# One GpSimd power over eight columns for two normalisations, in an attention and feed-forward kernel

## What is computed

```
def _layernorm(x, axis=-1, eps=1e-05):
    m = jnp.mean(x, axis=axis, keepdims=True)
    v = jnp.var(x, axis=axis, keepdims=True)
    return (x - m) / jnp.sqrt(v + eps)
...
q = (x @ Wq.T + bq).reshape(B, S, H, Dh)
v = (x @ Wv.T + bv).reshape(B, S, H, Dh)
...
scores = jnp.einsum('bhsd,bhtd->bhst', q, q) / jnp.sqrt(jnp.float32(E))
same = (b_hs[:, :, :, None] == b_hs[:, :, None, :]).astype(scores.dtype)
coeff = NB - 2 + same
attn = jax.nn.softmax(scores * coeff, axis=-1)
out = jnp.einsum('bhst,bhtd->bhsd', attn, v)
...
x = x + _layernorm(_L0_attn_ref(_layernorm(x, axis=-1), ...), axis=-1)
x = x + _layernorm(_L0_ffn_ref(_layernorm(x, axis=-1), ...), axis=-1)
```

## Time and profile before

| | us |
|---|---|
| median of 3 runs | 1428.81 |
| lowest and highest | 1426.63, 1431.72 |
| the profiled execution | 1425.1 |
| its span, first to last instruction | 1423.3 |
| GpSimd busy | 1257.9 (88%) |
| TensorE busy | 1236.9 (87%) |
| VectorE busy | 1236.4 (87%) |
| ScalarE busy | 1068.1 (75%) |

### The profile page before, as it was taken

One profiled execution on the slowest core, in us unless ns is written; L12 is line 12 of the kernel. 1 busy time (PEld: TensorE's weight loads), 2 busy tenths in 40 slices (PEclk: granted clock), 3 DMA queues, 4 the chain that ended last, 5 costly groups with the idle time before them and its releaser, 6 DMA issues. The chain is left out here.

```text
span 1423.3 us, 19971 instructions
## 1 busy us (share of the span) xinstructions
PE 1236.9 (87%) x5423; PEld 520.1 (37%) x5520; DVE 1236.4 (87%) x4005; ACT 1068.1 (75%) x1461; POOL 1257.9 (88%) x305
## 2 busy tenths in 40 slices
PE   2666799999989999898989999898999989898896
PEld 1111234334343434334343433434343433433343
DVE  3978999999999999999899999999999999999420
ACT  2244787878787887978788787878788797878741
POOL 2689999999999999999999999999999999999810
PEclk9877999999999999999999999999999999999999
DMA  3454345443543555354544544444454545443100
GB/s 99 135 172 127 109 121 152 114 133 113 144 116 115 136 128 137 94 148 117 140 104 128 146 116 135 111 144 117 113 141 116 142 100 142 117 129 92 47 8 8
DMA packets 89377, 167.47 MB, mean 118 GB/s; under 512 B 18096, under 2 KB 54192, under 8 KB 89264
## 3 DMA queue, kind: packets, MB, share of 16 engines
q1 hardware_dynamic: 89264, 166.19, 43.0%
HBM read 150.66 MB, written 15.47 MB: 117 GB/s over the span
## 5 line engine op out<-in xcount | busy, mean ns | idle before, releaser
L901 POOL TENSOR_TENSOR logits<-max_row,logits 128x4096 f32<-128x4096 f32 x128 | 1140.0, 8916 | 47.1 <-DMA max_row<-max_scratch 24.4
L730 DVE CUSTOM_DVE_ANT_0 logits<-s_bank,coeff 128x512 f32<-128x512 f32 x1024 | 692.3, 676 | 0.0
L940 ACT ACTIVATE logits<-logits 128x1024 f32<-128x1024 f32 x512 | 506.2, 1048 | 50.6 <-POOL logits L901 49.2
L695 DVE TENSOR_SCALAR coeff<-brow,bcol 128x516 bf16<-128x516 bf16 x1024 | 480.6, 469 | 54.5 <-PE s_bank L511 26.9
L511 PE MATMUL s_bank<-mov_stack,stat_stack 128*128 128x512 bf16 x927 | 328.4, 395 | 71.3 <-DVE rowmax L730 59.5
L531 PE MATMUL aux_bank<-logits,v_pad 128*32 128x512 f32 x2048 | 252.9, 613 | 31.5 <-ACT logits L940 17.0
L636 PE MATMUL f_bank<-hid_a,h_sb 128*128 128x512 f32 x512 | 248.9, 593 | 1.1 <-DVE hid_a L819 0.8
L511 PEld LDWEIGHTS s_bank<-mov_stack,stat_stack 128*128 128x128 bf16 x1024 | 97.9, 98 | 414.2 <-DVE rowmax L730 215.5
L646 PE MATMUL f_bank<-hid_b,h_sb 128*128 128x512 f32 x512 | 243.5, 593 | 5.0 <-ACT hid_b L1039 3.6
L960 ACT COPY oT<-aux_bank 128x512 f32<-128x512 f32 x64 | 37.5, 586 | 154.7 <-PE aux_bank L531 148.5
L646 PEld LDWEIGHTS f_bank<-hid_b,h_sb 128*128 128x128 f32 x512 | 95.9, 190 | 84.9 <-issue 73.0
(11 more groups left out here) (96 smaller groups left out, 961.3 us busy)
## 6 DMA issues: line engine op xcount, KB each, us to landing
max_row<-max_scratch SPq DMA_DIRECT2D x128, 512.0 KB, 4.1
brow<-bucket_scratch SPq DMA_DIRECT2D x64, 522.0 KB
mov_stack<-q_scratch SPq DMA_DIRECT2D x192, 96.0 KB
stat_stack<-q_scratch SPq DMA_DIRECT2D x192, 96.0 KB
max_scratch<-rowmax_T SPq DMA_DIRECT2D x512, 1.0 KB
q_scratch<-q_parts SPq DMA_DIRECT2D x16, 384.0 KB, 6.5
x_in<-in_x SPq DMA_DIRECT2D x16, 256.0 KB, 4.4
q_scratch<-q_parts SPq DMA_DIRECT2D x16, 256.0 KB, 7.2
```

Of the source, the lines that this page charges most:

```text
L695: nc.vector.tensor_scalar(coeff[:, k % 3, :].rearrange("p (r n) -> p r n", r=ROW_RUNS), brow[:, h // 4 % 2, h % 4, :, 0:RUN], bcol[:, b % ...
L730: nc.vector.tensor_tensor_reduce(out=logits[:, ring(b, k), :], in0=tile_bank(k)[:], in1=coeff[:, k % 3, 0:SEQ], scale=float(E) ** -0.5, sc ...
L901: nc.gpsimd.tensor_tensor(tiles, max_row[:, m % 2].unsqueeze(2).broadcast_to([P, GROUP, ST, SEQ]), tiles, ALU.subtract).then_inc(below_max ...
L940: nc.scalar.activation(logits[:, first:first + 2, :], logits[:, first:first + 2, :], ACT.Exp, scale=-1.0).then_inc(probs_done, 1)
```

## The change

GpSimd no longer takes the power for x at slot 48 and the one for the end at slot 52. It takes one at slot 52, over a tile of 8 columns, of which 0 to 3 are x's and 4 to 7 the end's; the product with the negated means is one over 8 columns too. Where an iteration only prepares or only finishes, the slice has 4 columns. GpSimd waits for both variances ahead of it. ScalarE's x normalise moves from slot 49 to slot 52, behind the exponential of that slot. One count of a semaphore, `xe_bias_done`, stands for both products.

```diff
-X_RSTD_SLOT = 48
-X_NORM_SLOT = 49
+X_RSTD_SLOT = 52
+X_NORM_SLOT = 52
...
-END_RSTD_SLOT = 52
...
-        minus_half = sb("minus_half", [P, ST])
+        minus_half = sb("minus_half", [P, 2 * ST])
...
-        x_var = sb("x_var", [P, ST])
-        x_rstd = sb("x_rstd", [P, ST])
-        x_shift = sb("x_shift", [P, ST])
-        x_bias = sb("x_bias", [P, ST])
+        xe_var = sb("xe_var", [P, 2 * ST])
+        xe_rstd = sb("xe_rstd", [P, 2 * ST])
+        xe_shift = sb("xe_shift", [P, 2 * ST])
+        xe_bias = sb("xe_bias", [P, 2 * ST])
...
-            def rstd(var, shift, out_, bias, prepared, done, bias_done, n):
-
-                pool.wait_ge(prepared, n)
-                nc.gpsimd.tensor_tensor(out_[:], var[:], minus_half[:], ALU.pow).then_inc(done, 1)
+            def rstd(var, shift, out_, bias, done, bias_done, n, part):
+
+                nc.gpsimd.tensor_tensor(out_[:, part], var[:, part], minus_half[:, part], ALU.pow).then_inc(done, 1)
                 pool.wait_ge(done, n)
-                nc.gpsimd.tensor_tensor(bias[:], shift[:], out_[:], ALU.mult).then_inc(bias_done, 1)
+                nc.gpsimd.tensor_tensor(bias[:, part], shift[:, part], out_[:, part], ALU.mult).then_inc(bias_done, 1)
...
-                    if query and k == X_RSTD_SLOT:
-                        rstd(x_var, x_shift, x_rstd, x_bias, x_var_done, x_rstd_done, x_bias_done, p + 2)
-                    if finish and k == END_RSTD_SLOT:
-                        rstd(end_var, end_shift, end_rstd, end_bias, end_var_done, end_rstd_done, end_bias_done, g + 1)
+                    if (query or finish) and k == X_RSTD_SLOT:
+                        if query:
+                            pool.wait_ge(x_var_done, p + 2)
+                        if finish:
+                            pool.wait_ge(end_var_done, g + 1)
+                        part = slice(0 if query else ST, 2 * ST if finish else ST)
+                        rstd(xe_var, xe_shift, xe_rstd, xe_bias, xe_rstd_done, xe_bias_done, i + 3, part)
...
                 if k == X_NORM_SLOT:
-                    act.wait_ge(x_bias_done, p + 1)
-                    normalise(x_in, x_in, x_rstd, x_bias, xn_done)
+                    act.wait_ge(xe_bias_done, p + 1)
+                    normalise(x_in, x_in, xe_rstd, xe_bias, xn_done)
...
                 if slot == END_NORM_SLOT + TILES:
-                    act.wait_ge(end_bias_done, f + 1)
-                    normalise(ffn, ffn, end_rstd, end_bias, end_normed_done)
+                    act.wait_ge(xe_bias_done, f + 5)
+                    normalise(ffn, ffn, xe_rstd[:, ST:2 * ST], xe_bias[:, ST:2 * ST], end_normed_done)
```

More of the change, by code:

```diff
@@ L222, in sandwich_kernel @@
         end_mv = sb("end_mv", [P, ST, 2])
[L223 to L226, removed]
         ynT = sb("ynT", [P, SEQ])
@@ L245, in sandwich_kernel @@
         x_var_done = sem("x_var_done")
-        x_rstd_done = sem("x_rstd_done")
-        x_bias_done = sem("x_bias_done")
+        xe_rstd_done = sem("xe_rstd_done")
+        xe_bias_done = sem("xe_bias_done")
         xn_done = sem("xn_done")
@@ L291, in sandwich_kernel @@
         end_var_done = sem("end_var_done")
-        end_rstd_done = sem("end_rstd_done")
-        end_bias_done = sem("end_bias_done")
         end_normed_done = sem("end_normed_done")
@@ L917, in iteration @@
                         nc.gpsimd.tensor_tensor(ffn[:], ffn[:], y1[:, g % 2], ALU.add).then_inc(y2_done, 1)
-                    if query and k == X_RSTD_SLOT:
-                        rstd(x_var, x_shift, x_rstd, x_bias, x_var_done, x_rstd_done, x_bias_done, p + 2)
-                    if finish and k == END_RSTD_SLOT:
-                        rstd(end_var, end_shift, end_rstd, end_bias, end_var_done, end_rstd_done, end_bias_done, g + 1)
+                    if (query or finish) and k == X_RSTD_SLOT:
[5 more added lines that the diff above has]
+                        rstd(xe_var, xe_shift, xe_rstd, xe_bias, xe_rstd_done, xe_bias_done, i + 3, part)
                     if feed and k == ATT_RSTD_SLOT:
-                        rstd(att_var, att_shift, att_rstd, att_bias, att_var_done, att_rstd_done, att_bias_done, 2 * f + 1)
+                        pool.wait_ge(att_var_done, 2 * f + 1)
+                        rstd(att_var, att_shift, att_rstd, att_bias, att_rstd_done, att_bias_done, 2 * f + 1, slice(0, ST))
                     if feed and k == Y1_RSTD_SLOT:
-                        rstd(att_var, att_shift, att_rstd, att_bias, att_var_done, att_rstd_done, att_bias_done, 2 * f + 2)
+                        pool.wait_ge(att_var_done, 2 * f + 2)
+                        rstd(att_var, att_shift, att_rstd, att_bias, att_rstd_done, att_bias_done, 2 * f + 2, slice(0, ST))
             stages(pool, iteration)
@@ L945, in prepare @@
                 act.wait_ge(ready, n)
-                nc.scalar.activation(var[:], mv[:, :, 1], ACT.Identity, bias=eps[:])
-                nc.scalar.activation(shift[:], mv[:, :, 0], ACT.Identity, scale=-1.0).then_inc(done, 1)
+                nc.scalar.activation(var, mv[:, :, 1], ACT.Identity, bias=eps[:])
+                nc.scalar.activation(shift, mv[:, :, 0], ACT.Identity, scale=-1.0).then_inc(done, 1)
             def normalise(dst, src, rstd, bias, done):
@@ L963, in query_step @@
                 if k == X_PREPARE_SLOT:
-                    prepare(x_mv, x_var, x_shift, x_mv_done, x_var_done, p + 1)
+                    prepare(x_mv, xe_var[:, 0:ST], xe_shift[:, 0:ST], x_mv_done, x_var_done, p + 1)
                 if k == X_NORM_SLOT:
-                    act.wait_ge(x_bias_done, p + 1)
-                    normalise(x_in, x_in, x_rstd, x_bias, xn_done)
+                    act.wait_ge(xe_bias_done, p + 1)
+                    normalise(x_in, x_in, xe_rstd, xe_bias, xn_done)
                 if k == XNT_COPY_SLOT:
@@ L1009, in ffn_step @@
                 if slot == ATT_PREPARE_SLOT:
-                    prepare(att_mv, att_var, att_shift, att_mv_done, att_var_done, 2 * f + 1)
+                    prepare(att_mv, att_var[:], att_shift[:], att_mv_done, att_var_done, 2 * f + 1)
                 if slot == Y1_PREPARE_SLOT:
-                    prepare(att_mv, att_var, att_shift, att_mv_done, att_var_done, 2 * f + 2)
+                    prepare(att_mv, att_var[:], att_shift[:], att_mv_done, att_var_done, 2 * f + 2)
                 if slot == END_PREPARE_SLOT + TILES:
-                    prepare(end_mv, end_var, end_shift, end_mv_done, end_var_done, f + 1)
+                    prepare(end_mv, xe_var[:, ST:2 * ST], xe_shift[:, ST:2 * ST], end_mv_done, end_var_done, f + 1)
                 if slot == ATT_NORM_SLOT:
```

## The result

The changed kernel took 1441.86 us (median of 6 runs, 1440.03 to 1442.41) against 1429.24 before: ratio 1.0094, 95% interval 1.0077 to 1.0111 (the two medians alone give 1.0088). Its profiled execution took 1440.82 us, where the one before took 1425.1. It is slower by 0.9%, where 1.1% was forecast.

A forecast was written before the change was run, and what follows sets the result against it. The prediction took ScalarE, VectorE and DMA, not GpSimd, as the path ahead of the maxima wait. 12 x 1.18 + 0.9 = 15.1 us on 1428.8 gave 1443.9 us, own range 1438 to 1449, wider range 1434 to 1449.

The forecast's parts named there:

- What bounds the kernel: Between about 745 and 771 us the path is ScalarE, VectorE, DMA; GpSimd runs beside it with room.
- Part 1: GpSimd, slots 48 and 52: merged power takes 1.8 us, relieving 5 to 15 us over the run, worth nothing in time.
- Part 2: GpSimd at slot 52 waits for both variances: no wait, 0.8 us to spare.
- Part 3: ScalarE's x normalise, slot 49 to 52: of 1.54 us, 0.36 absorbed before xnT, 1.18 passed on in each of 12 iterations.
- The idle at line 767: VectorE's wait for qT (old line 774) grows from 0.66 to 1.84 us, 12 times; under 1.5 means wrong.
- Part 4: The rest: iteration 1 is 0.9 us late; GpSimd's final addition, iteration 0 and iterations 14 on add nothing.
- The sum: Whole run: 12 x 1.18 + 0.9 = 15.1 us slower, giving 1443.9 us, slower by 1.1%.
- A: GpSimd is the bound, so its saving comes out: 5 to 15 us faster, 1414 to 1424; chance 0.06.
- B: VectorE's late start is absorbed by stalls after 771: 0 to 4 us, 1425 to 1433; chance 0.11.
- C: The lateness is partly absorbed, half of it: 1434 to 1438 us; chance 0.08.
- D: Late transposes of x leave 0.36 unrecovered, scores' lateness adds: 20 us, 1449; within the forecast's 0.75 as its upper end.

The follow-up runs named there:

- relief alone: Kernel before without the end's power and product on GpSimd in iterations 2 to 13, x normalise still at slot 49; 1429.07 us, ratio 0.9999.
- the two powers: Changed kernel with the merged power taken twice, the first into a tile nobody reads; 1444.13 us, ratio 1.0109 to the kernel before.
- the move alone: Kernel before with only ScalarE's x normalise moved from slot 49 to 52, GpSimd keeping its two powers; 1440.28 us, ratio 1.0088.

## Why the prediction was right

- **What bounds the kernel.** Right: GpSimd has the highest busy share and isn't the bound at this place. The run with relief alone shows it from below, the two powers from above. "At this place" matters: behind the maxima wait GpSimd runs to the next iteration with 1.82 us of idle in all, so for most of each iteration it is the path. The rule of the Trainium skill, Perfetto Trace Analysis, "Identifying the Most-Contended Engine", would have chosen GpSimd. The runs here agree with it only in part: 14.8 us less on that engine, taken off ahead of its wait, gave 0.
- **Part 1, the power.** 1.8 taken, 1.64 measured, inside the bounds of 1.01 and 1.82. GpSimd's busy time fell by 6.2 us (5 to 15 forecast). Worth nothing, as said.
- **Part 2, the new wait.** Right: line 943 began its end step at 756.23, GpSimd came at 757.50 and didn't wait.
- **Part 3, the move.** The steps came as told: oT copy idle 2.41 (2.4 told), the transposes of x 4.57 us after the copy where it was 4.58, no idle before xnT. The size was a little off: 1.08 us at xnT, where I had 1.18. I had spaced the exponentials 2.95 / 3 = 0.98 us, but an exponential's row is 1.06 long and the next starts 0.96 after it (760.92 to 761.88; two of them 1.89, 763.42 to 765.31). Three from 752.43 are then over at 755.28, and the idle before xnT at 755.74 that could be absorbed was 0.46, not the 0.36 in its bracket: 1.54 - 0.46 = 1.08. The Trainium skill, ScalarE: Activation LUTs, "What ACT_TABLE_LOAD costs", says that back-to-back activations overlap by about 93 ns; the 0.10 here agrees.
- **The idle at line 767.** 1.84 forecast, 1.22 measured. The prediction had called itself wrong if this idle came out under 1.5 us, and it did: its step that the whole delay would show there failed. The sum wasn't touched by it: 0.41 us of the delay was taken one score tile earlier, behind the query matmul. My sentence that VectorE's own wait would be later and longer held, but I hadn't taken the one from the other.
- **Part 4.** Iteration 1: 0.9 forecast. From its oT copy to line 774 it took 8.80 us before (190.25 - 181.45) and 9.45 after (191.65 - 182.20): 0.65. Iteration 0 was put at nothing, but line 767 came 0.33 us later after its oT copy there (9.04, before 8.71), which the move alone doesn't show (8.72). Where that comes from stays open.
- **The sum.** With the measured terms it is 12 x 1.06 + 0.65 = 13.4 us. The ratio of 1.0094 gives 13.4 of 1428.8 too, the medians differ by 12.6 and the profiled executions by 15.7, so a match to the tenth is luck. The forecast of 15.1 had the right terms, each a tenth or more too dear, and took the profiled execution to stand 3.7 us under the median again; it stood 1.0 under it.
- **The rivals.** A (a gain from GpSimd) and B (absorbed) didn't happen, nor C (half absorbed); D's condition, late transposes of x, didn't come either. Nothing was taken up later. The prediction gave as the reason that all four engines stand late together and showed no row behind 771; the rows above give a plainer one: from the maxima on, GpSimd has no idle but the same 1.82 us.

The version that beats both is the kernel before with qT ahead of the end normalise, 0.4 to 0.5% faster than before.

## What to carry to other kernels

When a merge makes one step wait for another's place in the queue, price the consumer's move first: here the saving was on an engine that waited behind it anyway, and the 1.5 us step that had to follow it left an idle gap on ScalarE and landed in front of work for which first VectorE, then the maxima and then GpSimd waited. An engine can be the path for most of an iteration and still have room just where the work is saved. Compare both traces from one event that the change doesn't touch, such as the copy of oT, and a delay can be followed step by step to 0.1 us. If taking a wait away returns less than its length, look at what else stands behind the late work in the same queue, and who waits for it.

## What the hardware showed

A GpSimd power over 128 x 4 numbers took 1.02 us and over 128 x 8 took 1.64, while the product of the same shapes took 0.20 both times. Merging two powers of four columns so saves 0.4 us and one product, not a whole power. If the time grows evenly with the columns, which two sizes can't show, the 0.62 us of difference leave about 0.4 fixed, by that estimate.
